# A semaphore for each kind of load in the tail, and the shared expert by half blocks behind two pairs of maxima at the head of attention

## The reference

```
xn = layernorm(x)
x  = x + linear_attention(xn) + fp6_quantized_linear(xn)
xn = layernorm(x)
x  = x + L1_attn(xn) + L1_ffn(xn)
# L1_attn: xn' = LN(xn, g1, beta1); q, k (rotary), v = xn' @ W + b; 16 heads of 16
#          x1 = xn + softmax(q k^T / 4) v @ Wo + bo
#          x1 + relu(LN(x1, g2, beta2) @ W1 + b1) @ W2 + b2
# L1_ffn:  shared = gelu(xn @ Wfc_s + bfc_s) @ Wproj_s + bproj_s        (width 1024)
#          plus the two best of 8 experts for each token, gated
```

## Time and profile before

| | us |
|---|---|
| median of 3 runs (4231.51 to 4236.89) | 4233.71 |
| the profiled execution's own time | 4234.2 |
| its span, first to last instruction | 4232.4 |
| TensorE busy | 4045.8 |
| VectorE busy | 3147.5 |
| ScalarE busy | 2713.9 |

### The profile page before, as it was taken

How to read it: one execution, slowest core, us unless ns; L and a number is a source line. 1 busy time by engine, 2 the same in 40 slices (tenths; PEclk the granted TensorE clock), 3 DMA queues, 4 the chain that set the end, 5 groups by cost and what they waited for, 6 DMA issues and landing times. The chain is left out here.

```text
span 4232.4 us, 74482 instructions
## 1 busy us (share of the span) xinstructions
PE 4045.8 (96%) x27844; PEld 1866.3 (44%) x27844; DVE 3147.5 (74%) x4621; ACT 2713.9 (64%) x5153; POOL 370.7 (9%) x435
## 2 busy tenths in 40 slices
PE   6988788999999999999999999999999999997799
PEld 4666543222222222222222222222226888875566
DVE  6888568999999999999999999999960111132432
ACT  4555414888888888888888888888895232321112
POOL 0222332001101100000000000000000000011110
PEclk8999899999999999999999999999999999999899
DMA  4222464000014100003100002000002666632320
GB/s 157 80 87 89 144 127 68 26 19 18 22 34 67 53 21 4 4 7 55 32 7 4 4 6 75 4 6 4 4 6 86 220 213 209 213 123 69 90 60 31
DMA packets 213030, 269.66 MB, mean 64 GB/s; under 512 B 25152, under 2 KB 176448, under 8 KB 211168
## 3 DMA queue, kind: packets, MB, share of 16 engines
q1 hardware_dynamic: 200368, 236.85, 19.3%
q0 software_dynamic: 12336, 28.48, 2.5%
HBM read 188.43 MB, written 76.55 MB: 63 GB/s over the span
## 5 line engine op out<-in xcount | busy, mean ns | idle before, releaser
L1346 ACT ACTIVATE a_PT<-a_PS 128x512 f32<-128x512 f32 x4096 | 2163.7, 606 | 347.7 <-PE a_PS L1141 317.4
L1489 DVE TENSOR_REDUCE a_MX<-a_PS 128x1 f32<-128x512 f32 x2958 | 1889.1, 685 | 21.4 <-PE a_PS L1122 5.5
L1152 PE MATMUL a_OT<-a_PT,a_VG 128*32 128x512 f32 x8192 | 1093.0, 605 | 1.1 <-ACT a_PT L1346 0.7
L1484 DVE TENSOR_REDUCE a_MX<-a_PS 128x2 f32<-128x1024 f32 x569 | 692.1, 1218 | 25.9 <-PE a_PS L1122 24.9
L1141 PE MATMUL a_PS<-p_Q,p_K 64*128 64x512 bf16 x4096 | 688.6, 379 | 9.3 <-DVE a_MX L1489 7.4
L1141 PE MATMUL a_PS<-a_QS,h_K 64*128 64x512 bf16 x4096 | 675.3, 378 | 0.5 <-ACT a_PT L1346 0.5
L1122 PE MATMUL a_PS<-h_K,a_QS 64*128 64x512 bf16 x2048 | 505.0, 379 | 0.6
L1122 PE MATMUL a_PS<-p_K,p_Q 64*128 64x512 bf16 x2048 | 498.7, 381 | 3.8 <-DVE a_MX L1484 2.7
L1141 PEld LDWEIGHTS a_PS<-p_Q,p_K 64*128 64x128 bf16 x4096 | 226.7, 94 | 604.4 <-DVE a_MX L1489 266.0
L1141 PEld LDWEIGHTS a_PS<-a_QS,h_K 64*128 64x128 bf16 x4096 | 220.8, 94 | 590.3 <-ACT a_PT L1346 270.3
L1650 ACT ACTIVATE e_hT<-e_up,p_Q 128x256 f32<-128x256 f32 x312 | 147.7, 473 | 394.2 <-PE e_up L1604 394.0
(11 more groups left out here) (238 smaller groups left out, 3425.8 us busy)
## 6 DMA issues: line engine op xcount, KB each, us to landing
p_K<-Wfc SPq DMA_DIRECT2D x26, 1024.0 KB, 5.0
p_K<-Wproj SPq DMA_DIRECT2D x26, 1024.0 KB, 7.1
p_Q<-Wfc SPq DMA_DIRECT2D x13, 1024.0 KB, 5.4
p_Q<-Wproj SPq DMA_DIRECT2D x13, 1024.0 KB, 7.5
scr_xs<-f_zero SPq DMA_DIRECT2D x1, 9984.0 KB, 33.1
p_Q<-scr_xs SPq DMA_DIRECT2D x39, 256.0 KB, 2.7
scr_ys<-e_Y SPq DMA_DIRECT2D x39, 256.0 KB, 2.2
scr_va<-f_va SPq DMA_DIRECT2D x8, 1024.0 KB, 4.9
```

The costliest lines, as they stand in the source:

```text
L1152: last = T.matmul(OT[w, :], VG[j][:, u, w], PT[:, (n * CHUNKS + HG * u + i) % RING, :], start=u == 0, stop=u == KT - 1)
L1346: nc.scalar.activation(PT[:, at % RING, :], bank, ACT.Exp, scale=SOFT_SCALE).then_inc(S["exp_done"], 1)
L1484: V.tensor_reduce(MX[n % 2][:, :, x], PS[:, bank:bank + SIDES, :], AX.X, ALU.max).then_inc(S["mp_free"], SIDES)
L1489: V.reduce_max(MX[n % 2][:, side, x:x + 1], PS[:, bank, :], AX.X).then_inc(S["mp_free"], 1)
```

## The change

In the tail each kind of load of the blocks from 2 on has a semaphore of its own (`sum`, `xn`, `res`, `xt`, one for even and one for odd blocks), each reader waits for its kind alone (`there`), and each kind is issued when its own buffer is free, in the order SUM/DEN, XN1, xT, the store of block i-2, RES. The load of xT is left out for blocks 2 and 3, which don't read it.

At attention's head the shared expert works on half blocks (256 tokens): a step is one up projection of a slice (two 128x256 matmuls into bank 6) and the down projection of the slice before (two 128x256 matmuls into `OT`). The 48 steps are cut 13, 32 and the rest: ahead of the pairs, behind two pairs each, and in the lead. The pairs use three sets of two banks instead of two. The transposition of the shift stands behind the second pair of the lead instead of ahead of the first.

```
-HEAD_BANKS = ((0, 1), (2, 3))
+HEAD_BANKS = ((0, 1), (2, 3), (4, 5))
...
+            def shared_up(g):
                 m, i = g % HC, g // HC
+                if g:
+                    pe.wait_ge(S["sh_hid"], g)
+                half = slice(i % 2 * SHALF, (i % 2 + 1) * SHALF)
+                for k in range(DC):
+                    last = T.matmul(PS[:, SHARED_UP, 0:SHALF], early["wfs"][:, k, m * P:(m + 1) * P],
+                                    early["xT"][i // 2][:, k, half], start=k == 0, stop=k == DC - 1)
+                last.then_inc(S["sh_up"], 1)
...
+            def shared_down(g):
                 m, i = g % HC, g // HC
+                pe.wait_ge(S["sh_hid"], g + 1)
                 if m == 0 and i:
+                    pe.wait_ge(S["sh_y"], i)
...
+            def shared_step(g):
+                if g < STEPS:
+                    shared_up(g)
+                if 0 < g <= STEPS:
+                    shared_down(g - 1)
...
-            for x in range(PAIRS):
+            for x in range(0, PAIRS, 2):
                 head_pair(x, SIDES * x, 0, 0, x)
-                shared((SHARED_LOAD + x,))
+                head_pair(x + 1, SIDES * (x + 1), 0, 0, x + 1)
+                shared_step(SHARED_LOAD + x // 2)
...
-            negmax_transpose(HEAD_TURN, 0)
...
             for x in range(LEAD):
-                if x == 0:
+                if x == 2:
+                    negmax_transpose(HEAD_TURN, 0)
                     pe.wait_ge(S["negmaxT_copied"], 1)
                 head_pair(PAIRS + x, SIDES * (PAIRS + x), 0, 1, x)
...
+                if x % 2 and x > 1:
+                    shared_step(SHARED_TURN + x // 2 - 1)
...
             for i in range(2, NB):
+                j = i % 2
+                sp.wait_ge(tt["att_ready"], (i - 1) * DC)
+                for G in range(NG):
+                    load_sums(sp, scr, tt, i, G, tt[f"sum{j}"])
+                sp.wait_ge(S["w_drained"], 2 * (i - 1))
+                load_block(sp, scr, tt, i, "XN1", "xn1", tt[f"xn{j}"])
+                if i not in SHARED:
+                    if i - 2 not in SHARED:
+                        sp.wait_ge(S["a_filled"], use_up(i - 2, HC - 1) + 1)
+                    load_turned(sp, scr, tt, i, tt[f"xt{j}"])
                 put(i - 2)
-                tail_rows(sp, scr, tt, i)
+                load_block(sp, scr, tt, i, "RES", "resid", tt[f"res{j}"])
...
-                    dve.wait_ge(*rows_load(tt, i + 1))
+                    dve.wait_ge(*there(tt, "sum", i + 1))
```

More of the change, by code:

```diff
@@ L1259, in last_block @@
                     weigh(n, u)
-            def shared_up(g, k):
+            def shared_up(g):
                 m, i = g % HC, g // HC
[L1263 to L1268, removed]
@@ L1290, in _ @@
+                for t in range(2):
+                    last = T.matmul(OT[:, t * D:(t + 1) * D], hT[:, g % SHR, t * P:(t + 1) * P],
+                                    early["wps"][:, m, :], start=m == 0 and t == 0, stop=m == HC - 1 and t == 1)
+                last.then_inc(S["sh_down"], 1)
+            def shared_step(g):
[3 more added lines that the diff above has]
+                    shared_down(g - 1)
             pe.wait_ge(early["load"], 16 * (3 + len(SHARED)))
-            shared(range(SHARED_SORT))
+            for g in range(SHARED_SORT):
+                shared_step(g)
@@ L1727, in tail_weights, with there @@
         eng.dma_start(dst[:], src).then_inc(tt["w_load"], 16)
-def rows_load(tt, i):
-    return (tt[f"early{i}"], TAIL_IN * 16) if i < 2 else (tt[f"load{i % 2}"], i // 2 * TAIL_IN * 16)
-def tail_rows(eng, scr, tt, i, ready=lambda k: None):
-    j, n = i % 2, slice(i * BLK, (i + 1) * BLK)
-    there = rows_load(tt, i)[0]
+def there(tt, name, i):
+    if i < 2:
+        return tt[f"early{i}"], TAIL_IN * 16
+    each = 2 * NG if name == "sum" else 1
+    rows = [n for n in range(2 + i % 2, i + 1, 2) if name != "xt" or n not in SHARED]
+    return tt[f"{name}{i % 2}"], len(rows) * each * 16
@@ L1738, in tail_rows, with load_turned, first_rows @@
+def load_turned(eng, scr, tt, i, sem):
+    eng.dma_start(tt["xT"][i % 2][:], scr["xn1T"][:, i * BLK:(i + 1) * BLK].rearrange("(c p) n -> p c n", p=P)).then_inc(sem, 16)
+def first_rows(eng, scr, tt, i, ready):
+    sem = tt[f"early{i}"]
     for G in range(NG):
-        rows, k = slice(G % 2 * HALF, (G % 2 + 1) * HALF), G // 2
-        heads = scr["att"][G].rearrange("(h w) n -> h w n", h=HG)
         ready(2 * G)
-        eng.dma_start(tt["SUM"][j][rows, k, :], heads[:, 0:HD1, n]).then_inc(there, 16)
@@ L1743, in tail_rows @@
-        eng.dma_start(tt["DEN"][j][rows, k, :], heads[:, HD1:HD1 + 1, n].to_broadcast([HG, HD1, BLK])).then_inc(there, 16)
-    for k, (name, src) in enumerate((("XN1", "xn1"), ("RES", "resid"))):
-        ready(2 * NG + k)
-        eng.dma_start(tt[name][j][:], scr[src][n, :].rearrange("(t p) c -> p t c", p=P)).then_inc(there, 16)
-    eng.dma_start(tt["xT"][j][:], scr["xn1T"][:, n].rearrange("(c p) n -> p c n", p=P)).then_inc(there, 16)
+        load_sums(eng, scr, tt, i, G, sem)
+    ready(2 * NG)
```

66 lines of the change are left out of this document (35 added, 31 removed).

## The result

| | before | after |
|---|---|---|
| median, us | 4233.12 (4231.51 to 4236.89, 4 runs) | 4173.06 (4171.65 to 4174.93, 4 runs) |
| the profiled execution's own time, us | 4234.2 | 4171.98 |
| its span, us | 4232.4 | 4170.2 |

The ratio of the runs is 0.9857 with a 95% interval of 0.984 to 0.9874: faster by 1.4%. The medians differ by 60.1 us, the two profiled spans by 62.2 us. To see where, cut each span at points that both have: the first unit of the shared expert, the first pair, the end of the 64th maximum, the first score (L1141 before, L1140 after), and the first `project` of the tail.

What follows compares the result with a forecast made beforehand. The prediction took TensorE as nearly always busy, its large load-caused wait being 44.4 us for attT in the tail. Tail -50.5 and head -12.1 sum to -62.6, so 4171 us by the median; range 4163 to 4185.

Steps and rivals of the forecast that it cites:

- Tail, the waits: Tail: all three waits of TensorE for attT go, -44.4 us.
- Tail, the slow projections: Tail: three projections no longer run at the low clock, 2.0 us each, 6.1 us less in all.
- Tail, the margin: Tail: attT is ready 1.4 us before TensorE reaches project, at each of two blocks.
- The rival that the margin isn't there: Tail: VectorE's operations or block 3's sums come some 4 us late twice, +8 to +14, about 4182 us; 7%.
- Tail, the diagnosis: Tail: SUM and DEN are late only through issue behind block 0's store and waiting together with xT; eleven loads took 20.9 us.
- Head, the pairs: Head, 64 pairs: 32 periods of 2.45 us instead of 2.76, -9.9 us, bounds -15.7 and -3.5.
- Head, the start: Head, before the pairs: waiting for the first GELU and its table costs +1.2 us net, bounds 0 and +2.5.
- Head, the lead: Head, 64th maximum to first score: VectorE goes on without a break, -3.4 us, bounds -4.1 and -2.4.
- VectorE as the bound: Rival, head's pairs: VectorE sets the pace at a period of 2.27 us, head -17, 4166 us; 6%.
- the head gives little: Rival, head: second pair 0.41 us after the first, late clock rise, fall in the lead; head -3.4, 4180 us; 20%.
- the slower one: Rival, head's pairs: short, frequent waits keep TensorE's clock low, period about 4.8 us, 4256 us in all; 2%.
- SyncE's queue: Rival, tail: the store between two blocks' loads holds them back as before; the tail gives nothing, 4221 us; 2%.

Runs made afterwards that it cites:

- tail_only: The changed kernel with the head of the kernel before, so only the tail's edits: 4182.37 us, ratio to before 0.9879.
- sems_only: The changed kernel with the tail's old order of issue, xT of blocks 2 and 3 included, keeping a semaphore per kind: 4213.15 us, ratio to before 0.9948.
- one_behind_each: The changed kernel with the up projection behind the first pair and the down projection behind the second: 4182.41 us, one run.
- two_sets: The changed kernel with two sets of banks for the pairs instead of three, and the transposition in bank 4: 4181.68 us, one run.
- Best: The changed kernel with two alternating up banks before the pairs and, for tail blocks 1 to 3, a down projection behind Z's transposition: 4166.5 us, ratio to before 0.9841.
- turn_first: The changed kernel with the transposition of the shift ahead of the lead's first pair again: 4178.64 us, one run.
- sems_plain: sems_only with SUM and DEN loaded from whole rows of another tensor, as many bytes and loads: 4194.26 us, ratio to before 0.9911.
- order_only: The changed kernel with one semaphore for all loads of a tail block, keeping the new order and the two omitted xT loads: 4185.73 us, ratio to before 0.9883.

## Why the prediction was right

It forecast 4171 and 62.6 us less; measured were 4173.06, 60.1 us less by the medians, and 62.2 less by the profiled spans, on which its terms are laid out. Step by step:

- **Tail, the waits.** -44.4 forecast, and all three waits are gone. tail_only shows that they go by the tail's edits alone.
- **Tail, the slow projections.** -6.1 forecast; 3 x 3.62 - 16.95 = -6.1 measured. The first `project` was 1.2 longer (6.55 for 5.38), which I had not foreseen and which comes from the clock behind the barrier, told above. Together -49.8 for -50.5; -44.4 - 6.1 + 1.2 is -49.3, and the other half a microsecond is the modelled end (0.16 each) of the matmul ahead of each wait, which the waits leave out.
- **Tail, the margin.** 1.4 us forecast, 1.5 measured, and VectorE's list of waits in the tail has no load in it. The rival that the margin isn't there fell.
- **Tail, the diagnosis.** Here a step was wrong without harm: "Neither SUM nor DEN is late for a reason of its own". sems_only showed that the sums alone take 16.1 of the 20.9 us. The forecast held because it bounded block 3's sums by the whole 20.9 against 32 us of lead time; had I forecast the semaphores without the new order in the same way, I would have missed by 18 us, as the expectation for sems_only did.
- **Head, the pairs.** A period of 2.45 forecast, 2.46 measured, and -9.5 for -9.9 by the end of the 64th maximum. The price of 0.31 for both changes was right (0.30 by one_behind_each). The choice between 2.45 and 2.65 hung on the third set of banks, and two_sets, with periods of 2.47 and 2.69 in turn, confirms it.
- **Head, the start.** +1.2 forecast, +2.2 measured, within the bounds 0 and +2.5. The idle time was near the count (1.91 for 2.2), but the choice that the clock would rise at the same moment as before was wrong: it rose 3 us later. Best shows the reverse, a rise that comes earlier with the idle time gone.
- **Head, the lead.** -3.4 forecast, -4.2 measured, just past the bound of -4.1. I had expected part of the low clock to stay, since TensorE "stands still about as long now". It stood still for 0.88 and 0.35 us in place of 1.48 and 0.54, with two pairs more ahead, and the clock stayed up to the last pair of the lead. turn_first puts the longer waits back and the clock falls. These two terms missed by +1.0 and -0.8, and that they made each other good was luck.
- **The rest.** The front, the loop and the experts moved by -0.2 and -0.8, for which nothing was forecast. In the rivals, the sum for VectorE as the bound is -15.7 + 1.2 - 3.4 = -17.9 and not -17, which makes 4165 of its 4166 and changes nothing.

Of the rivals, "the head gives little" needed 0.41 between pairs, a late rise and a fall in the lead; only the late rise came. VectorE did not become the bound of the pairs (busy 74.90 of 78.80), and the clock was 1.00 through them, so neither that rival nor the slower one came. SyncE's queue held nothing back.

## What to carry to other kernels

When one reader waits for several loads on one semaphore, measure how long the load that it needs takes by itself before blaming the one that came last. Here an earlier issue, with two loads left out, was worth 35 us and separate counting 12. Put the bf16 and the float32 matmuls into groups as large as the PSUM banks allow, and count the changes between them as work of TensorE, here 0.3 us for each there and back (the array's tiling changed with the type). When an edit moves a wait of a microsecond or more of TensorE, price the clock with it: here waits of 4 to 5 us cost a further 3 us each, and with one transposition two pairs later the clock stayed up and the head was 3 us shorter.

## What the runs showed of the hardware

- Loads of 64x512 float32 from 4 heads of 16 rows, or from 4 rows repeated 16 times, kept the DMA engines busy at a share of 0.27, at 94 GB/s; loads of as many bytes from 64 whole rows ran at a share of 0.78, at 227 GB/s (sems_only and sems_plain).
- Two pairs of bf16 matmuls and a step of float32 matmuls took 2.46 us with the pairs together and 2.77 with one pair ahead of each half of the step: 0.30 us for one more change there and back (after and one_behind_each).
- The granted clock fell to its low level after waits of TensorE of 4.02 and 4.72 us (order_only), but not after one of 1.59 us in the tail of sems_only (row below). In the lead it fell with waits of 1.53, 0.35 and 0.96 us close together (turn_first), and stayed up with 0.88 and 0.35 (after). Ahead of the first score it fell in one wait of 3.00 us (after).

```profile
3967.85 3.72 PE L1883 MATMUL u_w<-t_wo,t_attT 128*128 128x256 f32 x16 [1.59 <-DVE t_attT L1767]
```

- After the barrier ahead of the tail, equal code took 5.38 us in some executions and 6.5 to 6.6 in others for the first sixteen matmuls.
- The front of the program, which no kernel here changes, ended between 553.4 and 559.1 us in single executions. A difference of 1 to 5 us between two spans says little before both are cut at the same points.
